# Listing late rows in smaller turns and holding row loads to six groups ahead

## What is computed

```python
gate_scores = softmax(x @ Wg.T)                       # (tokens, 8)
topk_val, topk_idx = top_k(gate_scores, 2)            # shares, normed to sum 1
for e in range(8):
    h = x @ W1[e].T + b1[e]                           # (tokens, 512)
    a, b = split(h, 2)
    out += ((a * sigmoid(b)) @ Wo.T + bo) * comb[..., e]
x = x + gb * out
```

## Time and profile before

| | us |
|---|---|
| median of 3 runs | 728.73 |
| lowest and highest run | 724.88, 729.9 |
| the profiled execution | 725.47 |
| its span in the trace | 723.8 |
| mean granted TensorE clock | 0.94 |
| busy: TensorE, VectorE, GpSimd, ScalarE | 617.0, 602.9, 537.9, 523.0 |
| DMA traffic | 95.58 MB, mean 132 GB/s |

### The profile page before, as it was taken

How to read it: one execution, slowest core, us unless ns; L and a number is a source line. 1 busy time by engine, 2 the same in 40 slices (tenths; PEclk the granted TensorE clock), 3 DMA queues, 4 the chain that set the end, 5 groups by cost and what they waited for, 6 DMA issues and landing times. The chain is left out here.

```text
span 723.8 us, 14261 instructions
## 1 busy us (share of the span) xinstructions
PE 617.0 (85%) x3515; PEld 469.7 (65%) x3515; DVE 602.9 (83%) x1384; ACT 523.0 (72%) x1321; POOL 537.9 (74%) x657
## 2 busy tenths in 40 slices
PE   2556889999999999979789687737899999999994
PEld 0433566667777666648557565615688888888883
DVE  6389989999999999997999846665688888888884
ACT  2656668898888977976766676734677888788883
POOL 5467667899999779899869876575766666666666
PEclk8699989999999999998999899857999999999998
DMA  3999888889999898788778799525565444444420
GB/s 109 259 139 133 117 110 133 132 142 160 149 136 159 128 152 112 155 167 157 152 135 147 170 283 286 220 98 166 118 103 87 79 77 78 79 80 80 76 18 1
DMA packets 103300, 95.58 MB, mean 132 GB/s; under 512 B 14523, under 2 KB 82710, under 8 KB 102966
## 3 DMA queue, kind: packets, MB, share of 16 engines
q1 hardware_dynamic: 85846, 79.69, 58.3%
q0 software_dynamic: 16176, 12.75, 10.0%
q10 hardware_dynamic: 1200, 2.23, 0.9%
HBM read 35.47 MB, written 25.61 MB: 84 GB/s over the span
## 5 line engine op out<-in xcount | busy, mean ns | idle before, releaser
L2063 POOL DMA_INDIRECT out<-res,index x91 | 141.3, 1553 | 66.0 <-DVE res L2145 48.1
L843 POOL TENSOR_TENSOR rs_prod<-rT,state_rows 128x512 f32<-128x512 f32 x128 | 139.4, 1097 | 44.7 <-DVE state_rows L1528 43.2
L1281 PEld LDWEIGHTS ps_k<-w,gel 128*128 128x128 f32 x512 | 63.5, 205 | 16.8 <-issue 14.4
L1281 PE MATMUL ps_k<-w,gel 128*128 128x128 f32 x512 | 66.2, 291 | 2.4 <-ACT gel L1098 1.7
L2112 DVE SCALAR_TENSOR_TENSOR half<-ps_b,xg,sig 128x256 f32<-128x256 f32 x91 | 43.6, 480 | 26.0 <-ACT sig L1991 22.8
L1987 ACT ACTIVATE sig<-ps_a 128x256 f32<-128x256 f32 x91 | 35.1, 385 | 41.6 <-issue 20.7
L1246 PE MATMUL ps_f<-hnT_hi,mix_hi 128*128 128x512 f32 x128 | 54.7, 428 | 8.7 <-DVE hnT_lo L1651 7.6
L2105 DVE SCALAR_TENSOR_TENSOR ps_a<-ps_a,xg,sig 128x256 f32<-128x256 f32 x91 | 44.4, 488 | 10.8 <-ACT sig L1987 6.5
L1941 PEld LDWEIGHTS ps_y<-out_w,gT 128*128 128x128 f32 x364 | 47.3, 191 | 8.9 <-ACT gT L2020 5.2
L2013 ACT ACTIVATE ps_b<-bias_rows 128x512 f32 x89 | 53.0, 595 | 0.0
L1247 PE MATMUL ps_f<-hnT_lo,mix_hi 128*128 128x512 f32 x128 | 52.0, 406 | 0.0
(11 more groups left out here) (357 smaller groups left out, 1995.7 us busy)
## 6 DMA issues: line engine op xcount, KB each, us to landing
v_spread<-vT SPq DMA_DIRECT2D x128, 256.0 KB
xg<-sorted_scratch SPq DMA_DIRECT2D x91, 130.0 KB
xin<-in_L_attn_x SPq DMA_DIRECT2D x16, 256.0 KB, 6.3
x<-in_L_attn_x SPq DMA_DIRECT2D x16, 256.0 KB
out<-x SPq DMA_DIRECT2D x16, 256.0 KB
sorted_scratch<-gel SPq DMA_DIRECT2D x4, 910.0 KB, 8.0
tokens_scratch<-h SPq DMA_DIRECT2D x12, 256.0 KB
raw_w<-in_L_ffn_W ACTq DMA_DIRECT2D x2, 1024.0 KB, 8.1
```

The source lines that it names most:

```text
L843: pool.tensor_tensor(rs_prod[:, p, idx % 4], rT[p][:], state[idx][:, p * NT:(p + 1) * NT], ALU.mult).then_inc(s["rs_ready"], 1)
L1281: mm = pe.matmul(ps_k2[:, q * P:(q + 1) * P], gel[c][:, q * P:(q + 1) * P], w2[:, c, :], start=(c == 0), stop=(c == NF - 1))
L2063: pool.indirect_dma_start(out_rows, bass.IndirectOffsetOnAxis(ap=index[k % RESULTS][:, i:i + 1], axis=0), res[k % RESULTS][:, i, :], None, ...
```

## The change

The loads of groups 6 and later now wait, each by itself, for a product into ps_a: load j for product j - 5. The last sixteen rows are listed in turns of two and one. The first turn goes as before; turn j waits for j products into ps_a. There are eleven turns (2, 1, 2, 1, 2, 1, 2, 1, 2, 1, 1), so the last row waits for ten products.

```diff
-    FIRST_SEED = 2
+    FIRST_SEED, AHEAD = 2, 6
...
             def load_group(j):
                 k = j // 2
+                if j >= AHEAD:
+                    sp.wait_ge(s["a_ps"], j - AHEAD + 1)
                 if k >= LOADS and j % 2 == 0:
...
-            for part in range(4):
-                if part > 0:
-                    pool.wait_ge(s["a_ps"], 2 * part)
-                list_rows(RG + part * RG // 4, RG + (part + 1) * RG // 4)
+            first = RG
+            for j in range(RG):
+                if j > 0 and first < 2 * RG:
+                    pool.wait_ge(s["a_ps"], j)
+                end = min(first + (2 if j % 2 == 0 else 1), 2 * RG)
+                list_rows(first, end)
+                first = end
             for k in range(PAIRS):
```

## The result

| | before | after |
|---|---|---|
| median, us | 728.85 (5 runs) | 717.04 (5 runs) |
| lowest and highest run | 724.88, 730.09 | 714.01, 718.54 |
| the profiled execution | 725.47 | 718.54 |
| its span | 723.8 | 716.8 |

The ratio is 0.9838 with a 95% interval from 0.9804 to 0.9871: 11.8 us faster, where 2.6 was forecast. The two profiled executions differ by only 6.9 us.

A forecast was written before the change was run, and what follows sets the result against it. TensorE was taken to bound the expert stage, with gain possible only at its start. One of two pauses, 2.6 us, off the 728.73 us median, other parts priced 0, gave 726.1 us, range 721.5 to 732.0.

The forecast's parts named there:

- What bounds the kernel: Expert stage: TensorE sets the end at 4.62 us per pair; only the stage's start, 8.3 us above pace, can gain.
- the two places named: TensorE idle 2.57 us before ps_y at 504.53 and 2.64 us before the table product at 518.38, ScalarE late.
- other 3.1 us: Rest of the stage start's 8.3 us: table products, short issue gaps, beginning of pair 1's hand-over; said to stay unchanged.
- C's tail: Both TensorE pauses go and the remaining 3.1 us shrinks too: down to 721 us.
- the size of the gain: Start of expert stage: between nothing and 5.2 us; one of two pauses taken, 2.6 us, giving 726.1 us.
- rival C: Both TensorE pauses at the stage's start go, 5.2 us gained: 723.5 us; chance 0.12.
- DMA shares: DMA engines busy 0.46 in window 498 to 506 with a pause, 0.79 at 520 to 525 without; counted against dense issuing.
- Rival B: Nothing gained, 728.7 us: early-stage pauses wander or belong to the stage's code, such as code fetches; chance 0.33.
- The listing's arithmetic: GpSimd: last row about 523.5, first scatters about 524.5, backlog caught up at pair 12; price 0.
- The loads' gate at price 0: SyncE's 85 load waits cost nothing: cover 3.4 us before `turn(k)`, 3.0 us at group 16's hand-over.
- D's mechanism in its single form: A few late loads hold `turn(k)` from pair 8, one at group 16: 730 to 733 us; whole rival 0.15.
- D's regular form: Loads regularly late from pair 8 on, every pair losing half the excess: 9.5 us, 738 us; chance 0.05.

The follow-up runs named there:

- loads only: Kernel before plus only the wait in front of loads from 6 on, old listing of four parts of four rows kept; 728.38 us, ratio 0.9989.
- narrow extras: New listing in turns without the loads' gate, plus six extra listings of 64 values behind the first six rows; 730.14 us, ratio 1.0019.
- paced: Kernel before with sixteen rows listed singly, no product waits, GpSimd filling a spare tile three times between rows; 717.41 us, ratio 0.9861.
- sixteen in one run: Kernel before with all last sixteen rows listed in one run, no waits between them; 733.78 us, ratio 1.0062.
- wide ones: New listing in turns without the loads' gate, plus six extra listings of whole 260-value rows; 729.23 us, ratio 1.0007.
- fours spaced: Kernel before, four parts of four rows kept, later parts waiting for 3, 6 and 9 products instead of 2, 4, 6; 723.61 us, ratio 0.9956.

## Why the prediction was wrong

*What bounds the kernel* held: nothing behind pair 6 moved, and of the 6.9 us between the two profiled executions 5.99 lie in the five turns with the two places named and 0.92 in front of them. The "other 3.1 us" that the change was to leave alone shrank too: four turns took 20.74 us (496.87 to 517.61) and not 26.74, which is 6.0 less where the brackets were 5.2. (C's tail is 723.5 - 3.1 = 720.4, not 721. And the 1% taken for what a measurement can tell was wide: the interval of the result is 0.3% to either side.)

*The step that failed is the size of the gain,* "From above: both idle times, 5.2 us. I take one of the two, 2.6 us". The gain was 11.8 us. The step failed three times. First, one profiled execution was taken for the kernel. Its five turns were 31.4 us where the three other traces with the old listing have 34.8 to 36.3, in executions of 726.97 to 729.59 us; its 3.3 us under the median, which I noted, were most likely this. The kernel before was profiled only once, so that its own typical run looks like these three is inferred from their equal medians. I moved the sum over to the median instead of asking what the median run had more of. Second, both pauses went and not one; rival C, which had that, stood at 723.5 for the same reason, still 6.5 us too slow. Third, the idle of TensorE was priced at its own length; the lower granted clock behind it, 0.51 over 520 to 526 in loads only, wasn't in the sum, because the profile of before shows 1.00 there.

*The cause was half right.* That three engines paused together in a dense stretch was the right thing to see. I put it down to "loads 7 to 9 and rows 5 to 8" alike. The early loads are not what makes the pauses (held back alone, 0.9989 and 1.0007); the rows are, by their spacing. That the three engines "share nothing but the memory side" no run shows. The DMA shares that I counted against it (0.46 in the window with the pause) weren't evidence against it: the share says how busy the DMA engines are, and the narrow extras show that the bytes they move aren't what matters. Rival B, no gain, leaned on the same shares and on the spread of the runs.

*The listing's arithmetic held,* shifted with TensorE. Eleven turns were made; the last row left at 516.38 and not at 523.5, since the tenth product came sooner. Scatters began at 517.65 and caught up at pair 12 (562.73), as worked out. From the last row to load 16 it took 4.5 us (520.86), where 5.3 were taken. Nobody waited for a late scatter. Price 0 was right.

*The loads' gate at price 0* was right as a cost: SyncE waited 68.2 us for products and `turn(8)` and the later ones had their rows in time. The cover was as thin as said only for a list that ends later: paced paid 1.2 us at that very place, which is D's mechanism in its single form. D's regular form appeared nowhere.

*Not shown* is what lies between GpSimd's indirect DMAs and the slow queues of ScalarE and SyncE. Runs narrowed it to the count of indirect DMAs in time: not bytes, not GpSimd's work, not the row loads. Whether scatters can do it too no run tells: in the changed kernel they go 1.86 us apart from 517.65 to 562 without a pause, but that is a spacing on the safe side of 1.61. Code fetches, which I had set up as B's explanation, have no row at the first pause in any of the traces with the old listing, though they have one on each of two queues between 512 and 520. In sixteen in one run no fetch has a row anywhere from 496 to 520, the stretch with ScalarE's four idle times of 2.51 to 6.69 us. Only two queues moved anything there (packets, MB, share of 16 engines):

```profile
q0 software_dynamic: 723, 2.01, 22.7%
q1 hardware_dynamic: 1172, 1.09, 19.3%
```

So no arriving code ended any of those idle times, and B's explanation does not hold for them.

The Trainium skill (DMA: Bandwidth & Descriptors, SWDGE vs HWDGE vs iDMA) says that GpSimd writes two descriptors for each piece it moves into rings in SBUF. A count that matters where bytes don't (730.14 us with narrow extras, 729.23 with wide ones, 128 rows each) is what such writes would give; that they are what slows the other queues was not tried.

The rule of the Trainium skill that the prediction cites for D, that a completion increment lands only behind every earlier write of its DMA engine across its queues, stands in DMA: Bandwidth & Descriptors under Queues, rings and completion order. No run here shows it.

## What to carry to other kernels

When several engines show idle time at once with releasers that make no sense ("remote", a tensor that the stage doesn't touch), look at what GpSimd issues just then, and at the durations of the small steps in another engine's queue: 18 ns that became 700 is the sign. Spacing indirect DMAs by a third of a microsecond more (1.61 for 1.27) was worth about 11 us here, and spacing by time did it at least as well as spacing by waits. And before a single profile is priced, ask by how much it lies off its median; what the typical run has more may be the thing that the change removes.

## What was not expected of the hardware

- With indirect DMAs from GpSimd 1.27 or 1.35 us apart, in runs of eight or more, the queues of ScalarE and SyncE went slowly (steps of 0.7 us for 0.02 to 0.3, ScalarE idle for 3.4 to 6.7 us at a time); of the four runs of four in fours spaced, three passed and the last did not (4.62). With sixteen in a row 1.61 us apart there was none of it.
- Six extra ones of 64 values per row cost as much as six of 260 (730.14 and 729.23 us, 719.27 without).
- In loads only, each of two pauses of TensorE of 3 to 4 us was followed by the lower clock: 0.50 over 506 to 508, and 0.51 over 520 to 526, in which it was busy for 5.90 of 6 us.
